# Splitting half of a message sum into single-pass matmuls, packing block numbers, and sharing one-hot columns, in a graph-network kernel

## The reference

```python
def gnn(h, e, d2, ...):
    ei, ej = e[0], e[1]
    x = concatenate((h[ei], h[ej], d2), axis=-1)
    msg = silu(x @ mW1 + mb1)
    msg = layer_norm(msg, ln_g, ln_b)
    msg = silu(msg @ mW2 + mb2)
    agg = segment_sum(msg, ei, num_segments=3125)
    y = concatenate((h, agg), axis=-1)
    return h + silu(y @ uW1 + ub1) @ uW2 + ub2

x = x + gnn(layernorm(x), ...)
x = x + ffn(layernorm(x)[None], ...)[0]   # half of the rows, by a score, through a gelu layer
```

## Time and profile before

| | us |
|---|---|
| median of the runs (lowest, highest) | 2267.47 (2264.85, 2274.99) |
| profiled execution, its own time | 2273.0 |
| its span | 2271.0 |
| busy in the span: TensorE, VectorE, ScalarE, GpSimd | 1969.9, 1733.3, 1314.6, 1237.7 |

### The profile page before, as it was taken

One profiled execution on the slowest core, in us unless ns is written; L12 is line 12 of the kernel. 1 busy time (PEld: TensorE's weight loads), 2 busy tenths in 40 slices (PEclk: granted clock), 3 DMA queues, 4 the chain that ended last, 5 costly groups with the idle time before them and its releaser, 6 DMA issues. The chain is left out here.

```text
span 2271.0 us, 45335 instructions
## 1 busy us (share of the span) xinstructions
PE 1969.9 (87%) x11037; PEld 1679.3 (74%) x11038; DVE 1733.3 (76%) x4528; ACT 1314.6 (58%) x2595; POOL 1237.7 (54%) x1178
## 2 busy tenths in 40 slices
PE   3546674379999999999999999999999999799996
PEld 1324553267888888888888888888888888677775
DVE  5789999667778778778777787787787787436795
ACT  2322331256667777777776776777777677433331
POOL 7753222466666666666666666666666666503000
PEclk9987776589999999999999999999999999999998
DMA  3000000343333333333333333333333333010001
GB/s 123 0 1 21 26 26 18 102 136 124 87 87 95 92 87 93 97 87 94 96 93 86 94 96 87 91 95 93 90 94 95 88 92 92 1 40 2 27 1 57
DMA packets 107787, 165.05 MB, mean 73 GB/s; under 512 B 42141, under 2 KB 78330, under 8 KB 107485
## 3 DMA queue, kind: packets, MB, share of 16 engines
q0 software_dynamic: 42016, 111.40, 18.0%
q1 hardware_dynamic: 59822, 47.94, 6.8%
q10 hardware_dynamic: 5900, 5.08, 0.7%
HBM read 152.30 MB, written 11.65 MB: 72 GB/s over the span
## 5 line engine op out<-in xcount | busy, mean ns | idle before, releaser
L917 POOL DMA_INDIRECT g_rows<-b_table,idx_ring x792 | 763.3, 964 | 485.1 <-ACT act L967 277.8
L1048 PE MATMUL ps<-w2g,nT 128*128 128x256 f32 x3336 | 789.1, 379 | 0.0
L1048 PEld LDWEIGHTS ps<-w2g,nT 128*128 128x128 f32 x3336 | 601.5, 190 | 64.5
L956 ACT ACTIVATE normed<-act,shift,rstd_e 128x255 f32<-128x255 f32 x834 | 450.1, 590 | 16.1 <-DVE shift L1115 13.7
L1031 PE MATMUL psG<-msg,ohf 128*125 128x256 f32 x1668 | 429.9, 380 | 0.4 <-issue 0.4
L972 ACT ACTIVATE nT<-psM 128x512 f32<-128x512 f32 x417 | 248.7, 596 | 309.9 <-PE psM L1040 234.3
L1082 DVE TENSOR_TENSOR agg<-psG,agg 125x256 f32 x834 | 348.9, 418 | 88.2 <-PE psG L1031 30.9
L1022 PE MATMUL psH<-a_sb,ohT 128*128 x1668 | 348.1, 332 | 40.2 <-DVE ohT L1135 35.5
L1146 DVE TENSOR_TENSOR g_rows<-psH,g_rows 128x512 f32<-128x512 f32 x417 | 285.4, 684 | 67.2 <-issue 27.5
L1152 DVE BATCH_NORM_STATS2 stat_e<-act 128x6 f32<-128x256 f32 x834 | 311.0, 415 | 14.6 <-ACT act L967 14.6
L1022 PEld LDWEIGHTS psH<-a_sb,ohT 128*128 128x128 f32 x1668 | 260.1, 192 | 68.7 <-issue 48.4
(11 more groups left out here) (196 smaller groups left out, 1995.8 us busy)
## 6 DMA issues: line engine op xcount, KB each, us to landing
loc_rows<-loc_d SPq DMA_DIRECT2D x139, 187.5 KB
g_rows<-b_table,idx_ring POOLq DMA_INDIRECT x792
h_sb<-in_x SPq DMA_DIRECT2D x1, 3125.0 KB
b_table<-b_out SPq DMA_DIRECT2D x25, 125.0 KB
x_all<-in_x ACTq DMA_DIRECT2D x1, 3125.0 KB
out<-x_all SPq DMA_DIRECT2D x5, 625.0 KB
ohT<-ew_d SPq DMA_DIRECT2D x139, 9.0 KB
idx_ring<-rec SPq DMA_DIRECT2D x132, 3.0 KB
```

The costliest lines, as they stand in the source:

```text
L917: pool.indirect_dma_start(g_rows[:, j, n, :], None, b_table[:, :], bass.IndirectOffsetOnAxis(ap=which, axis=0)).then_inc(s_gather[j], 16)
L956: ins = nc.scalar.activation(normed[:, j % 2, n, 0:D - 1], act1[:, (j - 10) % RING, n, 0:D - 1], ACT.Identity, scale=rstd_e[:, g % 2, k:k ...
L1048: mm = pe.matmul(ps2[:, k, n, :], nT[:, k, n, q, :], w2g[:, q, :], start=(q == 0), stop=(q == 1))
```

## The change

- **Edges, tile 0 of each pair.** ScalarE writes its message twice: rounded to float32r (high, its own instruction of 256 columns), and, behind act1, in float32 back into ps2's bank (s_whole). VectorE subtracts at the end of the slot: low = ps2 - high, in float32r (s_low). TensorE sums tile 0 in two float32r matmuls, high and low, into the same psG bank. Tile 1 keeps its float32 matmul, with a 256-column msg. The order in psG is tile 1, high, wait for low, low.
- **Block numbers.** At the end of routing VectorE packs six 5-bit block numbers into a word (six_blocks, six linked instructions of one partition). It loads two registers per body instead of twelve and takes each number out by a shift and a mask before its add. TensorE's own load is unchanged.
- **shifts** moves from the head of VectorE's slot to behind ohf.
- **Routing.** or_ covers ten columns on VectorE. GpSimd makes the other three (orp, four buffers, in the place of f1 and f2), one tensor_scalar of 128 columns each: those of steps 0 to 3 before its jump chain, those of step s + 4 behind the scatter of step s. TensorE waits for both (s_orp).

Cut of the diff (allocations of buffers and semaphores that only follow from it are left out):

```diff
--- before.py
+++ after.py
@@ -33,6 +33,8 @@
 ROWS = TILES * P + P * WIN + P
 DG = PAIRS // RING
 EQR = 4
+PCOLS = 3
+PRING = 4
...
+        six_blocks = alloc(edge_mem, "six_blocks", [1, TILES // 6], I32)
...
-            or_ = sb("or_", [P, 2, COLS, P], BF16)
+            or_ = sb("or_", [P, 2, COLS - PCOLS, P], BF16)
+            orp = [half[:, k * PCOLS * P // 2:(k + 1) * PCOLS * P // 2].bitcast(BF16).rearrange("p (t r) -> p t r", t=PCOLS)
+                   for half in (f1, f2) for k in range(PRING // 2)]
             oqv = sb("oqv", [P, 2, COLS, PLANES, WIN], BF16)
             recw = sb("recw", [P, 4, WIN, 8], BF16)
             tri = sb("tri", [P, P], BF16)
@@ -511,6 +519,19 @@
                 pool.wait_ge(s_loc, 1)
                 pool.affine_select(out=vals[:, TAIL:EC, 0], in_=vals[:, TAIL:EC, 0], compare_op=ALU.is_gt, fill=0.0,
                                    base=FULL, pattern=[[0, EC - TAIL]], channel_multiplier=-1).then_inc(s_planes, 1)
+
+                def pool_columns(s):
+                    if s >= PRING:
+                        pool.wait_ge(s_win, s - PRING + 1)
+                    for k in range(PCOLS):
+                        c = s * COLS + COLS - PCOLS + k
+                        ins = pool.tensor_scalar(orp[s % PRING][:, k, :], iota_n[:, :], r_all[:, c:c + 1], None,
+                                                 ALU.is_equal)
+                    ins.then_inc(s_orp, 1)
+
+                pool.wait_ge(s_places, 1)
+                for s in range(PRING):
+                    pool_columns(s)
                 pool.wait_ge(s_upto, 1)
                 pool.tensor_tensor(upto[:, :, :], upto[:, :, :], tot[:, :, :], ALU.subtract).then_inc(s_jump, 1)
                 pool.wait_ge(s_jump, 1)
@@ -535,6 +556,8 @@
                     pool.wait_ge(s_recw, s + 1)
                     pool.indirect_dma_start(rec_d[:, :], bass.IndirectOffsetOnAxis(ap=dest[:, s:s + 1], axis=0),
                                             recw[:, s % 4, :, :].rearrange("p w n -> p (w n)"), None).then_inc(s_scat, 16)
+                    if s + PRING < SUPERS:
+                        pool_columns(s + PRING)
 
             @block.tensor
             def _(pe):
@@ -612,10 +635,12 @@
 
                 def route(s):
                     pe.wait_ge(s_or, s + 1)
+                    pe.wait_ge(s_orp, s + 1)
                     if s >= 3:
                         pe.wait_ge(s_recw, s - 2)
                     for t in range(COLS):
-                        mm = pe.matmul(psK[:, s % 3, 0:PLANES * WIN], or_[:, s % 2, t, :],
+                        marks = or_[:, s % 2, t, :] if t < COLS - PCOLS else orp[s % PRING][:, t - COLS + PCOLS, :]
+                        mm = pe.matmul(psK[:, s % 3, 0:PLANES * WIN], marks,
                                        oqv[:, s % 2, t, :, :].rearrange("p n w -> p (n w)"),
                                        start=(t == 0), stop=(t == COLS - 1))
                     mm.then_inc(s_win, 1)
@@ -715,7 +740,8 @@
                 link(V.tensor_scalar(f2[:, :], place[:, :], -(WIN / 2 - 0.5), MAGIC_W, ALU.add, ALU.add))
                 link(V.tensor_scalar(f2[:, :], f2[:, :], -MAGIC_W, None, ALU.add))
                 link(V.tensor_scalar(r_all[:, :], f2[:, :], 1.0 / WIN, None, ALU.mult))
-                link(V.tensor_tensor(q_all[:, :], place[:, :], f2[:, :], ALU.subtract))
+                V.tensor_tensor(q_all[:, :], place[:, :], f2[:, :], ALU.subtract).then_inc(s_places, 1)
+                dve.wait_ge(s_places, 1)
 
                 def flat(ap):
                     return ap.rearrange("p b s -> p (b s)")
@@ -740,8 +766,10 @@
                     if s >= 2:
                         dve.wait_ge(s_win, s - 1)
                     own = slice(s * COLS, (s + 1) * COLS)
-                    V.tensor_tensor(or_[:, s % 2, :, :], r_all[:, own].unsqueeze(2).broadcast_to([P, COLS, P]),
-                                    iota_v.unsqueeze(1).broadcast_to([P, COLS, P]), ALU.is_equal)
+                    mine = slice(s * COLS, (s + 1) * COLS - PCOLS)
+                    V.tensor_tensor(or_[:, s % 2, :, :],
+                                    r_all[:, mine].unsqueeze(2).broadcast_to([P, COLS - PCOLS, P]),
+                                    iota_v.unsqueeze(1).broadcast_to([P, COLS - PCOLS, P]), ALU.is_equal)
                     if s:
                         dve.wait_ge(s_or, s)
                     link(V.tensor_tensor(oq, q_all[:, own].unsqueeze(2).broadcast_to([P, COLS, WIN]),
@@ -782,6 +810,13 @@
                         dve.wait_ge(s_last_row, 1)
                         for k in range(2):
                             V.tensor_tensor(w2g[:, k, :], w2g[:, k, :], psC[:, D:2 * D], ALU.subtract).then_inc(s_centred, 1)
+                dve.wait_ge(s_tbl, 16)
+                sixes = tile_block[0:1, 0:TILES].rearrange("a (m i) -> a m i", i=6)
+                link(V.tensor_copy(six_blocks[0:1, :], sixes[:, :, 5]))
+                for i in reversed(range(5)):
+                    link(V.scalar_tensor_tensor(out=six_blocks[0:1, :], in0=six_blocks[0:1, :], scalar=5,
+                                                in1=sixes[:, :, i], op0=ALU.logical_shift_left, op1=ALU.bitwise_or))
+
                 for g in range(TG):
                     n = min(P, TILES - g * P)
                     dve.wait_ge(s_recT[g], 16)
@@ -804,12 +839,14 @@
             idx_ring = sb("idx_ring", [P, 2, RING], I32)
             loc_rows = sb("loc_rows", [NB, 2, RING // 2, 2 * P], BF16)
             ohT = sb("ohT", [P, RING, 2, P], F32R)
-            ohf = sb("ohf", [P, 2, 2, NB], F32)
+            ohf = sb("ohf", [P, 2, 2, NB], F32R)
             g_rows = sb("g_rows", [P, RING, 2, D], F32)
             act1 = sb("act1", [P, RING, 2, D], F32)
             normed = sb("normed", [P, 2, 2, D], F32)
             nT = sb("nT", [P, 2, 2, 2, P], F32)
-            msg = sb("msg", [P, 2, 2, D], F32)
+            msg = sb("msg", [P, 2, D], F32)
+            high = sb("high", [P, 2, D], F32R)
+            low = sb("low", [P, 2, D], F32R)
             var_e = sb("var_e", [P, 2, 6], F32)
             stat = sb("stat_e", [P, 2, 6, 2, 3], F32)
             delta = sb("delta", [P, 6], F32)
@@ -960,12 +1000,16 @@
                     if has(t, 13):
                         act.wait_ge(s_second, t - 12)
                         need(act, s_sum, t - 14)
-                        nc.scalar.activation(msg[:, (j - 13) % 2, :, :], ps2[:, (j - 13) % 2, :, :], ACT.Silu).then_inc(s_msg, 1)
+                        nc.scalar.activation(high[:, (j - 13) % 2, :], ps2[:, (j - 13) % 2, 0, :], ACT.Silu).then_inc(s_high, 1)
+                        nc.scalar.activation(msg[:, (j - 13) % 2, :], ps2[:, (j - 13) % 2, 1, :], ACT.Silu).then_inc(s_msg, 1)
                     if has(t, 4):
                         act.wait_ge(s_hid, t - 3)
                         need(act, s_norm, t - 9)
                         nc.scalar.activation(act1[:, (j - 4) % RING, :, :], g_rows[:, (j - 4) % RING, :, :],
                                              ACT.Silu).then_inc(s_act1, 1)
+                    if has(t, 13):
+                        act.wait_ge(s_high, t - 12)
+                        nc.scalar.activation(ps2[:, (j - 13) % 2, 0, :], ps2[:, (j - 13) % 2, 0, :], ACT.Silu).then_inc(s_whole, 1)
                     if has(t, 11):
                         act.wait_ge(s_nx, t - 10)
                         need(act, s_second, t - 12)
@@ -1027,8 +1071,10 @@
                         pe.wait_ge(s_msg, t - 13)
                         pe.wait_ge(s_ohf, t - 13)
                         need(pe, s_agg, 2 * t - 30)
-                        for n in range(2):
-                            mm = pe.matmul(psG[0:NB, k, n, :], ohf[:, k, n, :], msg[:, k, n, :], start=True, stop=True)
+                        pe.matmul(psG[0:NB, k, 1, :], ohf[:, k, 1, :].bitcast(F32), msg[:, k, :], start=True, stop=True)
+                        pe.matmul(psG[0:NB, k, 0, :], ohf[:, k, 0, :], high[:, k, :], start=True, stop=False)
+                        pe.wait_ge(s_low, t - 13)
+                        mm = pe.matmul(psG[0:NB, k, 0, :], ohf[:, k, 0, :], low[:, k, :], start=False, stop=True)
                         mm.then_inc(s_sum, 1)
                     if has(t, 11):
                         if isinstance(t, int) and t == 11:
@@ -1043,6 +1089,7 @@
                         k = (j - 12) % 2
                         pe.wait_ge(s_nT, t - 11)
                         need(pe, s_msg, t - 13)
+                        need(pe, s_low, t - 13)
                         for n in range(2):
                             for q in range(2):
                                 mm = pe.matmul(ps2[:, k, n, :], nT[:, k, n, q, :], w2g[:, q, :],
@@ -1062,19 +1109,23 @@
             @block.vector
             def _(dve):
                 V = nc.vector
-                regs = [dve.alloc_register(f"dve_block{n}") for n in range(2 * RING)]
+                packed = [dve.alloc_register(f"dve_six{n}") for n in range(2)]
```

(20 more changed lines are left out.)

6 lines of the change are left out of this document (added).

## The result

The changed kernel took **2342.07 us** (median of four, 2332.8 to 2350.38) against 2268.81 for the kernel before: a ratio of 1.032, interval 1.027 to 1.037. Slower, where 3% faster was forecast. Most of this document is about why the same two kernels, run later in another place, gave a ratio of 0.956.

A forecast was written before the change was run, and what follows sets the result against it. The prediction took TensorE to bound the edge stage and VectorE the routing stage. Edge stage 62 us less and routing 10 less took 2273 to 2201, or 2195 us from the median; range 2170 to 2225.

The forecast's parts named there:

- TensorE's part: Edge stage: float32r matmuls for tile 0 save 0.19 us per slot; slot becomes 3.31 us, body 19.9.
- VectorE's part: Edge stage: subtract adds 2.0, shorter register load gives back 2.1, register work adds 0.2; VectorE's body 20.0 us.
- ScalarE: Edge stage: three 256-column activations replace one of 512 columns; ScalarE needs 2.8 us of a 3.31 us slot.
- The new wait: TensorE waits for s_low inside psG; 1.8 us of play, so it costs little; 0.1 us of coupling per body.
- Slower: Rival, chance 0.05: register work delays each add by 0.17 us, TensorE waits for s_low every slot; 2340 us.
- About 0.6 us a body are waits: Edge stage: TensorE's 21.6 us body is 21.0 of work plus waits, carried over into the new 20.7 us body.
- GpSimd's work in this stage is unchanged, 66% of the time now and about 70% then: Edge stage: GpSimd's busy share rises only to about 70%, with no cost priced for it.
- Routing: Routing stage: or_ on ten columns saves 0.39 us a step, GpSimd keeps up; 10 us less in all.
- the pairs held by ScalarE's table copy: Routing: 6 of 21 pairs of steps, set by other engines, gain nothing; the other 15 would save 0.78 us each.
- the first ten steps: Routing: steps before dest is ready save 5 x 0.39 = 1.9 us.
- the contention of which I cited the Trainium skill: Routing: two-SBUF-input VectorE instructions, such as the scan, could be held by GpSimd's columns, 1.6 us together; gain then 8.4.
- TensorE's pace is reached in full: Rival, chance 0.20: VectorE stays under 19.9 us, loop-edge waits shrink; body 20.2, 97 us less there; 2150 to 2165 us.

The follow-up runs named there:

- j1_after: The changed kernel, unchanged, run on a chip where the kernel before takes about 2228 us: 2129.0 us, ratio 0.956.
- h3: Changed kernel with GpSimd's root first and gathers for slot t waiting for TensorE's psH of t-3, but the old psG without split: 2204.8 us.
- g1: Changed kernel with GpSimd's root ahead of its slot's gathers, and gathers for slot t also waiting for TensorE's psH of slot t-3: 2207.5 us, ratio 0.973.
- h4_gate_no_columns: Changed kernel with root first and gathers waiting for TensorE's psH, but VectorE building all 13 columns of or_: 15 us more than without that edit.
- j2_gate: Changed kernel with GpSimd's root first and gathers waiting for TensorE's psH, where the kernel before took 2227.4 us: 2126.6 us, ratio 0.955.
- the first four: Changed kernel without the split (2276.5 us), without the low chain (2358.1), with twelve registers loaded again, or with shifts back at the slot's head (2360.6).
- e8: Kernel before with one more, unused power of six columns on GpSimd per loop body: 2389.1 us, ratio 1.052.
- e9: Kernel before with GpSimd's wait for a free gather buffer taken once for three slots, meant to bunch six gathers: 3108.7 us.

## Why the prediction was wrong

**TensorE's part: right.** The slot is 3.30 us (forecast 3.31), low's float32r matmul 0.12 us.

**VectorE's part: right or too careful.** The load of two registers takes 0.53 us (forecast 0.6; by the Trainium skill, Runtime: NRT & Kernel Launch, section Instruction fetch mechanics, it would be 0.4, and the measurement decides). The forecast had VectorE's own body at 20.0 us; it fits into 19.81, busy 281 of 300 us.

**ScalarE: sized low.** In j1_after 274.5 of 300 us is 3.02 us a slot, not 2.8; it still fits into 3.30.

**The new wait: right.** With the gate and no bursts, taking the low chain away changes nothing (2129.9 against 2126.6). Its play vanishes only where TensorE's updates are held. The rival "Slower" put its loss into this wait, by register work. That its 2340 us is so near the 2342 measured is luck: the 42.7 us of this wait in after (42 waits between 700 and 1700 us) come with the bursts (j1_after has none of it), and no cost of the register work between the adds is to be seen.

**"About 0.6 us a body are waits": this step failed first.** I took 21.61 - 21.0 as ordinary waits of each body and carried it over. It was a mean over bodies of 21.0 and clusters of 24 to 26 us, as the starts of the 70 loads behind the earlier trace rows would have shown. On the chip without bursts before takes 41 us less, 0.6 x 69 (it wasn't traced there, but h3 with the old psG has bodies of 21.0).

**"GpSimd's work in this stage is unchanged, 66% of the time now and about 70% then": this step failed fatally.** Busy time leaves out the 0.30 us between gathers. With it GpSimd's own body is 12 x 1.25 + 2 x 1.36 = 17.7 us: 84% of 21.0, and 90% of 19.8. I weighed GpSimd only as an engine that might be late with its rows, and they are still asked for 10 us ahead of their use. What counted was how its gathers bunch, and TensorE's updates, which come up to 5 us late in this place. The stage lost 79.1 us where 62 were to be gained, and an edit to GpSimd's order and waits alone (g1) brings the kernel from some 2342 to 2207 us. No rival had it.

**Routing: larger than forecast.** 15.8 us in the profile (10 forecast); on the chips without bursts h4_gate_no_columns takes 15 us more than j2_gate by leaving it out. or_ went as forecast:

```profile
L770 DVE TENSOR_TENSOR or_<-x_all,psV 128x1280 bf16<-128x1280 f32 x48 | 70.9, 1476 | 0.0
L528 POOL TENSOR_SCALAR x_all<-iota_n,x_all 128x128 bf16<-128x128 bf16 x150 | 89.1, 607 | 2.3
```

1.48 us instead of 1.88, and 0.61 us a column (forecast 0.54). From step 10 to step 52 VectorE gained 18.4 us, 0.44 a step: the pairs held by ScalarE's table copy gain as well, which I had excluded. Against this the first ten steps lost 2.1 instead of gaining 1.9. The first twelve columns, 0.84 us each on average, began beside the scan:

```profile
159.83 3.39 DVE L749 TENSOR_TENSOR_SCAN agg<-agg 128x1550 f32<-128x1550 f32 x1
...
159.90 10.12 POOL L528 TENSOR_SCALAR x_all<-iota_n,x_all 128x128 bf16<-128x128 bf16 x12 [2.19 <-DVE x_all L743]
```

The average hides what happened. The first column alone, started 0.07 us after the scan, took 3.74 us, until 0.4 us after the scan's end; each of the other eleven took 0.61. The scan kept the 3.39 us of the earlier trace rows. So the trace agrees with the contention of which I cited the Trainium skill, only that GpSimd stood and not VectorE. VectorE stood at another place, for some 2.6 us, which the forecast didn't see. First before, then after:

```profile
178.35 0.61 DVE L778 TENSOR_SCALAR w2g<-w2raw,gcol 128x256 f32<-128x256 f32 x2
```

```profile
178.57 3.79 DVE L806 TENSOR_SCALAR w2g<-w2raw,gcol 128x256 f32<-128x256 f32 x2
```

The second of the two took 2.98 us instead of 0.35 (179.38 to 182.36), and GpSimd's tensor_tensor of L544 ran beside it (179.39 to 182.21), 5.5 us later than in before because of the twelve columns. In before another small one of VectorE was long beside the same chain (L767, 2.41 us, against 0.20 in after).

**By the chip without bursts.** The forecast's parts can be checked there: split against no split 2126.6 against 2204.8, 78 us, where (21.0 - 19.8) x 69.5 gives 83; routing 15. h3, which has all but the split, is 23 us faster than before there, so 8 us are left for the packing, the moved shifts and the gate together, which no run separates. Change in all 98 us, where the forecast had 72. The nearest rival is "TensorE's pace is reached in full", which has 107 to 117. It is right that VectorE stays under 19.9 us, and wrong in its reason for the rest: today's waits come from the bursts and not from the loop's edge.

**What stays open.** Why one chip holds TensorE's updates behind runs of gathers and another doesn't, and what made the kernel before 2359 us on the chip of the first four. The link between runs and bursts rests on their order in time in every trace that has bursts, on e8, where more work on GpSimd alone tripled the bursts, and on g1, where stopping GpSimd halved the stalls' length. Against it stands e9, with 134 runs of four and no late update. The path inside the chip was in no view. By the Trainium skill (TensorE: Matmul & The Clock Gate, section The cost: per-tile semaphore tail) TensorE's increments serialize at some 26 ns each; within after's bursts they come about 70 ns apart, and neither explains 5 us. By the Trainium skill (DMA: Bandwidth & Descriptors, section SWDGE vs HWDGE vs iDMA) GpSimd writes the descriptors of its DMAs into rings in SBUF; a ring coming round would fit a stop after every 104 gathers, but nothing here shows it.

## What to carry to other kernels

A mean per iteration hides its distribution: read the starts of one instruction per loop body first, and if most are at the bound's own pace and a few far off it, find what starts the few before pricing an edit to the bound. Count an engine that issues software DMAs with the pauses between issues, and when a bound is made faster, ask which engine's rhythm closes up, though its rows are still in time; here a wait that ties GpSimd's issue to TensorE's progress is worth 6% where updates are held (2345.7 to 2207.5, on chips where before took 2271 and 2270) and costs nothing elsewhere (2126.6 against 2129.0). And time a change of a few per cent on more than one chip and more than once, each time beside the kernel before: this one is 1.03 in one place and 0.956 in another, while with the gate it is 0.973 and 0.955, faster than before in both.
